# S4 resolvents two at a time, and Strassen sums of S3 and T3 with the other sign, in a fused S4 convolution and int4 SwiGLU kernel

## The reference

```python
g = einsum('bsh,ih->bsi', xn, Wg)          # Wg, Wu: 2752 x 1024, Wd: 1024 x 2752
u = einsum('bsh,ih->bsi', xn, Wu)          # all three from int4 words, a scale and a
ffn = einsum('bsi,hi->bsh', silu(g) * u, Wd)   # zero for each group of 64
# S4: one convolution kernel K of length 1024 for all rows
denom = g_l[:, None] - Lambda[None, :]     # 1024 roots of unity x 64 states
cauchy(v) = (v[None, :] / denom).sum(-1)   # four such sums: k00, k01, k10, k11
K = ifft(c * (k00 - k01 * (1 / (1 + k11)) * k10)).real
s4 = causal convolution of each row of xn with K, plus D[0] * xn
```

## Time and profile before

| | us |
|---|---|
| median of 3 runs | 1396.7 |
| the profiled execution's own time | 1395.57 |
| its span, first to last instruction | 1393.4 |
| PE busy | 1313.1 (94%) |
| VectorE (DVE) busy | 975.8 (70%) |
| GpSimd (POOL) busy | 687.9 |
| ScalarE (ACT) busy | 463.0 |

### The profile page before, as it was taken

The page is one execution under the profiler, slowest core; times in us unless marked ns, Lnnn a source line. Parts: engine busy times, 40 slices in busy tenths (PEclk is TensorE's granted clock), DMA queues, the critical chain, the costliest instruction groups (busy, mean ns, idle before and its releaser), DMA issues.

```text
span 1393.4 us, 17064 instructions
## 1 busy us (share of the span) xinstructions
PE 1313.1 (94%) x6302; PEld 623.3 (45%) x6302; DVE 975.8 (70%) x1036; ACT 463.0 (33%) x827; POOL 687.9 (49%) x483
## 2 busy tenths in 40 slices
PE   3688899999999999899999999899999999999998
PEld 2444344444444444344444444344444444444444
DVE  7966799999999998879999898524343433241432
ACT  5744544455444455344454543410000000000000
POOL 6772777878787777668788896620000000000000
PEclk8799999999999999999999999999999999999999
DMA  8111545454555445444645543999554345336331
GB/s 311 34 46 38 165 142 155 133 179 140 168 146 162 138 136 175 117 155 130 179 137 176 157 144 114 334 414 310 165 189 149 98 151 183 104 109 219 99 98 61
DMA packets 165168, 218.09 MB, mean 157 GB/s; under 512 B 42204, under 2 KB 122718, under 8 KB 163166
## 3 DMA queue, kind: packets, MB, share of 16 engines
q1 hardware_dynamic: 163646, 200.69, 46.4%
q10 hardware_dynamic: 1440, 16.32, 2.9%
HBM read 139.64 MB, written 77.34 MB: 156 GB/s over the span
## 4 chain that ended last, share of the span: by engine, by line
PE 57%; DVE 3%; issue 1%; ACT 1%; DMA 0%; POOL 0%; SPq 0%; ACTq 0%; DVEq 0%
PE px L1461 16%; PE px L1375 13%; PE pz L1461 8%; PE pz L1375 6%; PE pv L1488 6%; PE py L1461 4%; PE py L1375 3%; DVE wf L1575 1%; DMA w_d<-ds 0%; DVE wf L1546 0%; DVE wf L1543 0%; DVE wf L1617 0%; DVE hf L1673 0%; DVE hf L1676 0%; POOL ds L696 0%
## 5 line engine op out<-in xcount | busy, mean ns | idle before, releaser
L1375 PE MATMUL px<-xo,wo 128*128 128x512 f16 x2016 | 464.2, 384 | 28.0 <-ACT u L997 21.3
L1375 PEld LDWEIGHTS px<-xo,wo 128*128 128x128 f16 x2016 | 197.4, 99 | 273.9 <-issue 26.0
L687 POOL TENSOR_TENSOR wo<-wf,wo 128x512 f16<-128x512 f32 x147 | 235.9, 1614 | 70.4 <-ACT wo L943 70.4
L706 POOL TENSOR_TENSOR hs<-hf,hs 128x512 f16<-128x512 f32 x154 | 215.4, 1405 | 108.5 <-ACT hs L978 108.3
L1461 PE MATMUL px<-wd,hr 128*128 128x512 f16 x1056 | 232.3, 379 | 0.0
L1375 PE MATMUL pz<-xo,wo 128*128 128x512 f16 x1008 | 231.3, 379 | 0.1
L1461 PEld LDWEIGHTS px<-wd,hr 128*128 128x128 f16 x1056 | 102.3, 98 | 118.7
L1375 PEld LDWEIGHTS pz<-xo,wo 128*128 128x128 f16 x1008 | 98.6, 98 | 118.4 <-issue 0.4
L943 ACT ACTIVATE wo<-wf 128x512 f16<-128x512 f32 x147 | 91.6, 624 | 102.5 <-DVE wf L1547 92.5
L978 ACT ACTIVATE hs<-hf 128x512 f16<-128x512 f32 x154 | 94.5, 621 | 89.6 <-DVE hf L1639 47.6
L1461 PE MATMUL pz<-wd,hr 128*128 128x512 f16 x528 | 116.6, 379 | 0.0
(11 more groups left out here) (229 smaller groups left out, 1417.4 us busy)
## 6 DMA issues: line engine op xcount, KB each, us to landing
h_d<-hs SPq DMA_DIRECT2D x154, 256.0 KB, 2.6
hr<-h_d SPq DMA_DIRECT2D x56, 704.0 KB, 4.4
w_d<-ds SPq DMA_DIRECT2D x73, 256.0 KB, 2.1
wd<-w_d ACTq DMA_DIRECT2D x4, 2816.0 KB, 15.5
sz<-in_sz_gate SPq DMA_DIRECT2D x21, 512.0 KB, 5.1
sz<-in_sz_up SPq DMA_DIRECT2D x21, 512.0 KB, 4.8
sz<-in_sz_down SPq DMA_DIRECT2D x20, 512.0 KB, 5.1
xc_d<-xo SPq DMA_DIRECT2D x8, 1024.0 KB, 7.6
```

The lines of the kernel that those rows point to most:

```text
L687: pool.tensor_tensor(w_dest(t, j, 1), w_place_of(j), w_dest(t, j, 0), ALU.subtract).then_inc(wlo_done, 1)
L706: pool.tensor_tensor(hs[:, j, :, 1, :], h_place_of(p, j), hs[:, j, :, 0, :], ALU.subtract)\
L1375: done = pe.matmul(bank[:, :], wo[t % 2][:, j, wp, k * P:(k + 1) * P], xo[p][:, j, xp, k, :], start=(j in (0, 3) and k == 0 and wp == 0 an ...
```

## The change

Four things are edited.
1. **Resolvents by pairs.** Columns 2i and 2i+1 go through the same three ScalarE and seven VectorE instructions, now with 256 elements a partition, at units 6, 11, 16 and 21 (`RESOLVENT`). Their angles are loaded by `load_angles` (both rows, in groups 1 to 4). TensorE takes both columns two units later. Everything behind is one unit later: roots at 25, its transform in unit 26, and 27, 28, 29, 31, 32 for the rest.
2. **h.** S3 = A21 - A11 now, so that S2 = A22 + S3, and S1 = A21 + A22 and S2 are one instruction over [2, 512] with A22 broadcast (`h_s12`). The same signs on the side of x.
3. **Weights.** T3 = B12 - B22 now, so that T1 and T3 are one instruction with B12 broadcast, where T1 was (`t_sum`, `d_sum`). S3 times T3 is the same product. Semaphore counts follow (three sums for each tile, two for each slab of h).
4. **The tail.** The `and 15` of `tail_words` is a TENSOR_TENSOR with a broadcast tile `fifteen` set once by GpSimd.

```diff
+T_ORDER = (T1, T2, T4)
+T_POS = {T1: 0, T3: 0, T2: 1, T4: 2}
+RESOLVENT = (6, 11, 16, 21)
...
-            def load_angle(m):
+            def load_angles(i):
                 if i == 0:
                     sp.wait_ge(xt_done, 56)
+                else:
+                    sp.wait_ge(resolvent_done, i)
+                for h in range(2):
+                    m = 2 * i + h
+                    sp.dma_start(angle[:, h, :, :], angle_d[m:m + 1].broadcast_to((P, 2, P))).then_inc(angle_in[h], 16)
...
-                if g <= 4:
-                    load_angle(2 * g - 2)
+                if g <= 3:
+                    load_angles(g - 1)
...
-                if g <= 4:
-                    load_angle(2 * g - 1)
+                if g == 4:
+                    load_angles(3)
...
+            pool.memset(fifteen[:, :], 15).then_inc(below_done, 1)
...
             def scale_angles(n):
-                if n % 2 or not 6 <= n < 6 + 2 * M8:
+                if n not in RESOLVENT:
                     return
...
                 snap_s5(n + 1)
+                scale_angles(n + 1)
...
                 snap_s5(n + 3)
+                scale_angles(n + 3)
...
-                if n == 25:
+                if n == 26:
                     pe.wait_ge(roots_done, 1)
...
             def tail_words(kh, h):
+                dve.wait_ge(below_done, 2)
-                    link(dve.tensor_scalar(q[TAIL:P], r[TAIL:P], 15, None, ALU.bitwise_and))
+                    link(dve.tensor_tensor(q[TAIL:P], r[TAIL:P], fifteen[TAIL:P, :].broadcast_to((P - TAIL, 512)), ALU.bitwise_and))
...
             def t_sum(t, j):
                 if j == T1:
                     dve.wait_ge(deq_done, slab_up(t) + 1)
                     dve.wait_ge(wlo_done, base + W_POS[B11] + 1)
-                    dve.tensor_tensor(b11, b12, b11, ALU.subtract).then_inc(wsum_done, 1)
-                if j == T3:
-                    dve.tensor_tensor(b12, b22, b12, ALU.subtract).then_inc(wsum_done, 1)
+                    blocks = wf[:, :, :, :, :].rearrange("p s m n w -> p (s m n w)")[:, 0:10 * 256]\
+                        .rearrange("p (a b w) -> p a b w", a=2, b=5)
+                    dve.tensor_tensor(wf[:, 0, :, :, 0:256], wf[:, 0, 1:2, :, 0:256].broadcast_to((P, 2, 2, 256)),
+                                      blocks[:, :, 0:3:2, :], ALU.subtract).then_inc(wsum_done, 1)
...
             def h_s12(g, p):
                 dve.wait_ge(hf_done, 2 * n + 2)
-                dve.tensor_tensor(a21, a21, a22, ALU.add).then_inc(hsum_done, 1)
                 dve.wait_ge(hs3_done, q + 1)
                 dve.wait_ge(elo_done, 2 * q + 2)
-                dve.tensor_tensor(a, a22, a, ALU.subtract).then_inc(hsum_done, 1)
+                dve.tensor_tensor(hf[p][:, 0, :, :], hf[p][:, 0, :, :], hf[p][:, 1, 1:2, :].broadcast_to((P, 2, SB)),
+                                  ALU.add).then_inc(hsum_done, 1)
...
-                if n % 2 == 0 and 6 <= n < 6 + 2 * M8:
-                    resolvent((n - 6) // 2)
-                if n == 24:
+                if n in RESOLVENT:
+                    resolvent(RESOLVENT.index(n))
+                if n == 25:
                     cauchy_sums()
                     roots()
...
                 t_sum(2 * g + 1, T1)
-                t_sum(2 * g + 1, T3)
...
                 d_sum(g, T1)
-                d_sum(g, T3)
```

More of the change, by code:

```diff
@@ L253, in s4_plus_int4_swiglu @@
         below = small("below", [P, 1])
+        fifteen = small("fifteen", [P, 1], i32)
         par = small("par", [P, 5, 2])
@@ L267, in s4_plus_int4_swiglu @@
         ksc = small("ksc", [P, 3], i32)
-        angle = [at(f"angle{i}", [P, 2, P], f32, H0 + i * K1) for i in range(2)]
+        angle = at("angle", [P, 2, 2, P], f32, H0)
         flip = small("flip", [P, P])
         kshift = at("kshift", [P, 2, SB], f32, place[0])
-        s4w = small("s4w", [P, 4, P])
+        s4w = small("s4w", [P, 3, 2, P])
         dft = small("dft", [P, 2, P])
         twiddle = small("twiddle", [P, P])
+        zrow = at("zrow", [1, P], f32, place[0])
         krow = small("krow", [M8, 2, P // 2])
@@ L1395, in s4_steps @@
             def s4_steps(n):
-                if n % 2 == 0 and 8 <= n < 8 + 2 * M8:
-                    m = (n - 8) // 2
-                    pe.wait_ge(resolvent_done, m + 1)
-                    pe.matmul(pv[0][:, 8 * m:8 * m + 8], s4w[:, 2 + m % 2, :], vw[:, :], start=True, stop=True)\
-                        .then_inc(cauchy_done, 1)
-                if n == 25:
+                if n - 2 in RESOLVENT:
+                    i = RESOLVENT.index(n - 2)
+                    pe.wait_ge(resolvent_done, i + 1)
+                    for h in range(2):
+                        pe.matmul(pv[0][:, 16 * i + 8 * h:16 * i + 8 * h + 8], s4w[:, 2, h, :], vw[:, :], start=True, stop=True)\
+                            .then_inc(cauchy_done, 1)
+                if n == 26:
                     pe.wait_ge(roots_done, 1)
@@ L1722, in numerators, with resolvent @@
                 dve.tensor_scalar(sc[NS:P, 6:7], sc[NS:P, 2:3], -1.0, None, ALU.mult).then_inc(numer_done, 1)
-            def resolvent(m):
+            def resolvent(i):
                 dve.wait_ge(numer_done, 1)
-                dve.wait_ge(scaled_done, m + 1)
-                re, im, res = s4w[:, 0, :], s4w[:, 1, :], s4w[:, 2 + m % 2, :]
-                co, si = angle[m % 2][:, 0, :], angle[m % 2][:, 1, :]
+                dve.wait_ge(scaled_done, i + 1)
+                re, im, res = (s4w[:, k, :, :] for k in range(3))
+                co, si = angle[:, :, 0, :], angle[:, :, 1, :]
                 dve.scalar_tensor_tensor(out=im, in0=co, scalar=sc[:, 4:5], in1=im, op0=ALU.mult, op1=ALU.add)
```

76 lines of the change are left out of this document (33 added, 43 removed).

## The result

The changed kernel's median is 1403.9 us against 1396.3 us of the kernel before, 20 runs of each; the ratio on record is 1.0046 with a 95% interval of 1.0029 to 1.0062 (the two medians alone give 1.0054; the ratio of the means is 1.0046). The forecast was 1382 us and its range ended at 1390. The runs of the changed kernel lie in two clusters: 8 from 1392.75 to 1399.16 and 12 from 1403.44 to 1412.07. The 20 runs before lie within 2.7 us (1395.15 to 1397.81). The profiled execution, 1404.94 us, is of the upper cluster.

The account below looks back on a forecast made before the run. TensorE was taken as the bound, with gaps where VectorE is late. Losses of 44 us (13 + 2 + 14 + 7 + 8) would become 29.6, a gain of 14.5: 1381.1 for the profiled execution, 1382 us as median, range 1369 to 1390.

Parts of the forecast that it names:

- the last sentence on the tail: Start of phase B: the first load of h is next late, with a microsecond or so to spare.
- list of signs: What would show it wrong: VectorE full in group 3, a lump's gap over 5 us, phase B beginning with a load wait.
- The tail: End of phase A: L1575 falls from 7.14 to 1.64 us, and unit 43's loss of 8 us becomes 0.5.
- the second rival: Tail: GpSimd passes the new mask form too, 7.5 us of the gain goes, 1389.5 us; chance 0.15.
- the credit of 7.5 us: Tail: the gain counted for a mask without a stall, unit 43's loss going from 8 us to 0.5.
- The bound of 4.9 us: Tail: VectorE is 5.5 us earlier, cut to this because ScalarE's own instructions behind unit 41 stood at 877.6.
- Units 8 to 24: Resolvents by pairs: VectorE gives back 22 us, so TensorE's gaps there fall from 14 to 9.4 us.
- Unit 22: Behind the pair in unit 21: late `snap_s1` and `snap_u2` give TensorE gaps that add up to 3.6 us.
- The roots: Units 25 and 26: the wait at L1405 falls from 5.49 to 1 us; the loss becomes 4.6 instead of 7.
- Units 2 to 8: Early units: units 2 to 4 go from 13 to 13.2 us; the 2 us of units 5 to 7 are left.
- The sums: VectorE: merged sums of h take 2.0 us and of T1 and T3 1.9, saving 2.5 us in a group.
- The rival with all lumps exposed: Units 6 to 26: pairs and roots lie wholly on TensorE's path, 28 us more, 1410 us; chance 0.05.

Follow-up runs that it names:

- g3: f3 with the fourth and fifth Wd operand loads back ahead of ScalarE's last five h copies: 1388.5 us (1386.27 to 1402.15), ratio 0.9972.
- h3: The kernel before with only `snap_s1(43)` moved ahead of ScalarE's copies of T1, T2, S1 and S2: 1408.3 us, ratio 1.0083.
- f1: e4 with the tail's mask issued before VectorE's wait for the nibbles, beside GpSimd's memset: 1395.0 us, ratio 0.9989.
- f2: e4 with one more mask, over 128 partitions, ahead of the tail's mask on 32 partitions: 1396.9 us, one run.
- e2: The kernel before with only the other sign and the merged sums of h and weights: 1396.6 us, ratio 0.9995.
- g1: f3 with GpSimd's run of copies made to wait until VectorE's six instructions are done: 1387.7 us, ratio 0.9934.
- h1: f3 with `snap_s1(43)` moved ahead of ScalarE's copies of T1, T2, S1 and S2: 1387.9 us, ratio 0.9941.
- e4: The changed kernel with two Wd loads put behind ScalarE's last high halves and the landing of second-product h loads: 1395.1 us, ratio 0.9983.
- e1_pairs: The kernel before with only the resolvents by pairs and the roots one unit later: 1396.8 us, ratio 0.9991.
- f3: e4 with resolvents at units 6, 11, 15, 19, the roots in unit 23 and the later steps moved along: 1387.7 us, ratio 0.9932.
- e3: The kernel before with only the tail's `and 15` as TENSOR_TENSOR with the broadcast tile: 1397.0 us, ratio 0.9992.
- g2: The kernel before with only GpSimd's run of copies made to wait behind VectorE's six instructions: 1395.8 us, ratio 0.9995.
- f4: f1 and f3 together in one kernel: 1387.9 us, ratio 0.9936.

## Why the prediction was wrong

**The step that failed** is the last sentence on the tail: "Next late is the first load of h for phase B, issued after the same sums, with a microsecond or so to spare." The start of phase B was named, but the wrong load: the first landed in time, the second 0.6 us late, and the one that cost the time is the third, which SyncE issues when TensorE has ended phase A and not after the sums. It had 5.4 us to spare before the change (landed at 919.66, wanted at 925.04). And the sum put the start of phase B at nothing, which took the load's duration for fixed. It was 10.4 us in the one trace there was, and 25.8 to 28.6 in three others (the changed kernel, g3, h3); with the slow matmuls behind the wait that is 11.7 us. The trace of the kernel before had the warning: DMA share 1.03 in that stretch, and two loads of weights of 2.88 MB each queued for the same time, which at 421 GB/s is an estimate of 13.7 us for what they could take from this load; the waits measured are 9.2 to 11.7 us. The prediction's own list of signs ended with this wait; it had no chance and no price. With the 11.7 us the forecast would have been 1394, near no change.

**The tail** failed too, in two ways. L1575 was to fall from 7.14 to 1.64 us and rose to 9.63; the second rival, that GpSimd passes the new form too, was right. By the Trainium skill, "SBUF — State Buffer", section "Who interferes with whom", the shared port is held for a whole instruction by the one that issued first. The traces differ: eight GpSimd instructions pass one of VectorE whose record begins 0.02 us before the first of them. The same section says that the order of issue decides and not the shape, and f1 and f2 agree that the shape does not. It also says that a VectorE instruction with two SBUF inputs contends with GpSimd's reads, which the 9.63 us fit; but the old form, with one such input, took 9.36 us in e2. And the credit of 7.5 us for a mask without a stall is not borne out: g1 has no stall and wins nothing, though its copies start late by the edit. Behind the mask stood GpSimd's copies and the sums that need them (g1), ScalarE's order (h1), `snap_u2` (4.66 us in h1, 4.73 in h3) and the loads. The bound of 4.9 us that the prediction set came from ScalarE's row alone.

**Units 8 to 24** gave 2.1 us and not 5.0. The prediction's losses before add up to 44 us where its first paragraph has 43; the table has 45.7. Unit 12 (forecast 2.2, listed 1.82) and units 16 to 18 (3.2; 0.50 + 2.31 + 0.19 and small ones) were right in place and size. Unit 22 was forecast at 3.6 and cost 5.3: 3.89 of wait and 1.3 of slow matmuls (4.06 instead of 2.75). The resolvent lasts 8.8 us there (500.59 to `c12(21)` at 509.42), 8.7 forecast.

**The roots** were right in place: a wait of 1.17 at the transform (forecast 1) and one of 2.00 in unit 26. That the sum came near (5.2 against 4.6) is in part luck: the two waits with their 0.16 are only 3.5 us, and the rest is the slow matmuls (4.07) and small ones, which "pieces too short for a slow stretch" had excluded. In these traces a wait of 2.00 us behind one of 1.17 was enough, and in e4 one of 2.31 was followed by twelve at 4.44; in the changed kernel one of 2.31 was not (2.76).

**Units 2 to 8** lost 2.3 us more where the prediction left them as they were: the pair in unit 6 is the largest part of it (over units 2 to 8 e1_pairs lost 1.9 us more than the kernel before, e2_sums 0.6). Its lump shows as gaps in units 6 and 7 (1.66 and 1.29 us).

**The sums** were right or a little better than forecast: 1.82 and 1.70 us, forecast 2.0 and 1.9. VectorE's busy time fell from 975.8 to 947.2 us. The rival with all lumps exposed, the only slower case that was priced, played no part: e1 has them whole and costs nothing.

That VectorE was the cause of gaps and that lumps can be paid for was therefore sound, and f3 shows it: with the lumps in better units and the loads in a safe order, the change is worth 9.4 us (1387.7 against 1397.05), 0.68%. What stays open: what decides in a single run of the changed kernel or of g3 whether the load of h is late. Its issue stands in the same order to the others in all these traces, but not at the same distance. It comes 6.6 to 7.2 us behind SyncE's last store of h in the five where it took 9.6 to 11.2 us (before, e1, e2, e3, g2), and 4.7 to 5.3 us behind in the three late ones (the changed kernel, g3, h3). With the weights moved behind (e4, f1, f3, f4) it took 15.9 to 17.4 us at 5.2 to 5.5 us. No run moves this distance by itself. Open too is whether f3's gain would come without the merged sums; that was not tried.

## What to carry to other kernels

When a transfer that the next phase waits for has a margin of a few microseconds in a stretch where the DMA engines are full, treat its duration as unknown: give the case a chance of its own, and price it by the volume that the other queue may move meanwhile, not by the margin. Look at the size of the packets in both queues. Fix the order of the competing loads before you speed up what is in front of them. And before a stall on one engine is credited to the bound engine, remove it and see what the bound engine waits for then: here it was the copies, ScalarE's order and the loads in turn.

## What the runs showed of the hardware

- A VectorE instruction that begins within 0.02 to 0.07 us of the first of a run of ready GpSimd copies is passed by the whole run or most of it: 7.14 us before and in e1 and 7.40 in e3 (six), 9.36 in e2, 9.62 to 9.67 in the changed kernel, f1 and f2 (eight), for two shapes, the mask in both forms and a subtraction. One that begins in the middle of such a run takes turns with it (g1: 1.63 us, the copies 1.16 to 1.60). Why the moment matters is open.
- A DMA of 704 KB took 10.4 us in the kernel before and 25.8 to 28.6 in three kernels whose transfers are issued in the same order; from 905 to 935 us the kernel before moved 421 GB/s in all and the changed one 423. In one and the same program (g3) the late case came in 5 of 12 runs, by their times; one of them has a trace.
- Two full DMA queues move packet for packet: 126 and 124 packets in 6 us of the changed kernel, which is 2.53 and 0.06 MB.
- The reciprocal costs by its elements: 0.95 us for 128 and 1.75 for 256.
